# A small language-model block on one Trainium2 core: attention from fp32 heads on quarters of the array

## What is computed

```python
def _L0_attn_ref(x, qkv_w, qkv_b, proj_w, proj_b, q_norm_w, k_norm_w):
    qkv = x @ qkv_w.T + qkv_b                       # x: layernorm of h over the features
    q, k, v = split into 12 heads of 16
    q = rms_norm(q, q_norm_w);  k = rms_norm(k, k_norm_w)
    w = softmax(einsum('bhnd,bhmd->bhnm', q, k) / sqrt(16))
    out = einsum('bhnm,bhmd->bhnd', w, v)
    return out @ proj_w.T + proj_b                  # added to h
```

## Time and profile before

| | us |
|---|---|
| median of three runs (range) | 664.37 (664.18 to 664.48) |
| the profiled execution | 665.32 |
| its span, first to last instruction | 663.4 |
| mean granted TensorE clock, share of full speed | 0.928 |
| TensorE busy | 566.0 |
| VectorE busy | 377.8 |
| ScalarE busy | 271.9 |
| GpSimd busy | 84.3 |

### The profile page before, as it was taken

How to read it: one execution, slowest core, us unless ns; L and a number is a source line. 1 busy time by engine, 2 the same in 40 slices (tenths; PEclk the granted TensorE clock), 3 DMA queues, 4 the chain that set the end, 5 groups by cost and what they waited for, 6 DMA issues and landing times. The chain is left out here.

```text
span 663.4 us, 12309 instructions
## 1 busy us (share of the span) xinstructions
PE 566.0 (85%) x4521; PEld 460.8 (69%) x4521; DVE 377.8 (57%) x944; ACT 271.9 (41%) x787; POOL 84.3 (13%) x114
## 2 busy tenths in 40 slices
PE   6497896787999998988688777859988999999997
PEld 5386786764666666656376543548877999999996
DVE  2227648659899999988334653845662333223332
ACT  1123522344566666645325753514654222222220
POOL 5692000001000000000037400000100000000000
PEclk9799898999999999979687977967998999999999
DMA  9400000000000000000045002200003999999623
GB/s 316 121 1 2 0 1 1 0 1 1 1 2 1 1 0 0 1 1 1 1 171 223 1 1 84 96 0 1 2 1 124 404 311 313 306 318 309 217 47 108
DMA packets 20075, 57.90 MB, mean 87 GB/s; under 512 B 2804, under 2 KB 9574, under 8 KB 19911
## 3 DMA queue, kind: packets, MB, share of 16 engines
q1 hardware_dynamic: 14006, 48.04, 20.3%
q0 software_dynamic: 1024, 4.34, 3.6%
q10 hardware_dynamic: 4992, 4.82, 2.3%
HBM read 52.47 MB, written 4.33 MB: 86 GB/s over the span
## 5 line engine op out<-in xcount | busy, mean ns | idle before, releaser
L2048 DVE SCALAR_TENSOR_TENSOR ex_act_t<-banks,b_sb,ex_gelu 128x128 f32<-128x128 f32 x128 | 36.0, 344 | 95.4 <-ACT ex_gelu L2028 95.4
L2028 ACT ACTIVATE ex_gelu<-banks,b_sb 128x128 f32<-128x128 f32 x128 | 36.6, 368 | 100.7 <-PE banks L1979 100.7
L1974 PE MATMUL banks<-slots_t,w 128*128 128x128 f32 x512 | 62.5, 275 | 1.1 <-PEq L1670 1.1
L1974 PEld LDWEIGHTS banks<-slots_t,w 128*128 128x128 f32 x512 | 61.2, 192 | 1.4 <-issue 1.3
L1095 DVE TENSOR_REDUCE att_max<-banks 128x4 f32<-128x1024 f32 x48 | 58.6, 1220 | 2.6 <-PE banks L751 1.7
L945 ACT ACTIVATE att_prob<-banks 128x1024 f32<-128x1024 f32 x48 | 49.1, 1022 | 17.6 <-PE banks L774 17.6
L1992 PE MATMUL banks<-w,ex_act_t 128*128 128x192 f32 x256 | 50.2, 339 | 0.2 <-DVE ex_act_t L2048 0.2
L1992 PEld LDWEIGHTS banks<-w,ex_act_t 128*128 128x128 f32 x256 | 40.7, 189 | 4.3 <-DVE ex_act_t L2048 0.5
L1979 PE MATMUL banks<-slots_t,w 64*128 64x128 f32 x512 | 37.2, 285 | 0.0
L789 PE MATMUL banks<-att_prob,val 128*32 128x256 f32 x384 | 29.1, 426 | 7.2 <-ACT att_prob L945 7.0
L1187 POOL TENSOR_TENSOR att_qk<-att_qk,qk_weight 128x192 f32<-128x192 f32 x16 | 9.3, 600 | 203.8 <-DVE att_qk L1030 203.8
(11 more groups left out here) (233 smaller groups left out, 1144.0 us busy)
## 6 DMA issues: line engine op xcount, KB each, us to landing
w<-in_w SPq DMA_DIRECT2D x32, 768.0 KB, 7.7
w<-in_w2e SPq DMA_DIRECT2D x32, 384.0 KB, 8.6
w_slot<-in_w_slot SPq DMA_DIRECT2D x8, 576.0 KB, 3.8
rows_scratch<-ex_rows ACTq DMA_DIRECT2D x28, 96.0 KB, 6.5
yn_all<-rows_scratch POOLq DMA_DIRECT2D x7, 384.0 KB, 7.7
out<-h SPq DMA_DIRECT2D x8, 192.0 KB, 1.9
wq_t<-in_wq_t SPq DMA_DIRECT2D x1, 579.0 KB, 4.9
wk_t<-in_wk_t ACTq DMA_DIRECT2D x1, 579.0 KB, 5.4
```

What stands on the lines that cost most here:

```text
L1974: nc.tensor.matmul(bank[:, j * P:(j + 1) * P], g.w1[e][:, first + j * P:first + (j + 1) * P], x[:, 0, :], start=(j == 0), stop=False, skip ...
L2028: nc.scalar.activation(gelu[n % 2][:, j * P:(j + 1) * P], gate_bank(n)[:, j * P:(j + 1) * P], ACT.Gelu_apprx_tanh, bias=g.t["b1"][:, n, HB ...
L2048: nc.vector.scalar_tensor_tensor(out=act_t[n % 2][:, j * P:(j + 1) * P], in0=value_bank(n)[:, j * P:(j + 1) * P], scalar=g.t["b1"][:, n, j ...
```

## The change

The six bf16 parts are gone. The queries and keys of a head stay fp32, 16 features in a row of 32 columns (`g.qk`), and column 16 holds 1.0 for a key and, once `row_max` has run, the negated maximum for a query. A quad of four heads is then 128 columns, and one fp32 transpose lays head j on the partitions 32j to 32j+16. `fill_quad` has four such transposes a quad, for one bank of 128 x 512, and one copy a quad (ScalarE for quads 0 and 2, VectorE for quad 1). The scores are fp32 matmuls over 16 rows (for the maximum) or 17 rows (for the exponential), each on the quarter of the array's rows where its head lies. `scores_and_maxima` issues both kinds in turn, so that four matmuls in a row lie on four different quarters and write four different banks.

`split`, `split_rest`, `repeat` and `split_max` are removed on both engines. `turn_max` transposes the quad's 128 query columns again in fp32, and `keep_max` copies 128 x 256.

The 192 features of x are split as 128 + 64: three transposes of 128 columns give each tile its 128 and, in the third, the last 64 of both tiles on the two halves of the rows. The row of ones takes the place of feature 191: features of a normed row sum to zero, so GpSimd subtracts the weights' last row from all (`qkv_last`, in `token_mixer`), and the bias is loaded into the freed row by two DMAs that the attention stage waits for (`qkv_bias_set`). `keep_qk` is the two squares. Two operands, `qkv_w` (128 x 1728) and `qkv_last` (128 x 576), are loaded at the start in place of `qkv_t`.

The loops are written out in full, x is normalised two sequences ahead and not three, and the queries and keys are made one sequence ahead and not two. In the front part before body(0) only sequence 0 is made ready, with sequence 1's x; before, sequences 0 and 1 were made. The filler matmuls are at other places.

In the diff the first `body` is TensorE's, the second ScalarE's.

```diff
-            def max_scores(n, s, q, u):
-                pe.wait_ge(S["maxed"], 2 * count + u)
-                for hh in range(2):
-                    h = QH * q + 2 * u + hh
-                    for t in range(TPS):
-                        last = nc.tensor.matmul(g.ps[hh][:, t * SEQ:(t + 1) * SEQ],
-                                                q_t[s][0:KS, h, t * P:(t + 1) * P], k_t[s][0:KS, h, :],
-                                                start=True, stop=True)
...
+            def scores_and_maxima(score, best):
+                if score:
+                    n, q, u = score
+                    count = 2 * (QUADS * n + q) + u
+                    if u == 0:
+                        pe.wait_ge(S["max_kept"], QUADS * n + q + 1)
+                    if count:
+                        pe.wait_ge(S["exped"], count)
+                if best:
+                    bn_, bq, bu = best
+                    count = 2 * (QUADS * bn_ + bq) + bu
...
+                    if count:
+                        pe.wait_ge(S["maxed"], count)
+                for half in range(TPS):
+                    if best:
+                        for hh in range(2):
+                            row = 32 * (2 * bu + hh)
+                            last_best = nc.tensor.matmul(
+                                g.ps[MAXES[hh]][:, half * SEQ:(half + 1) * SEQ],
+                                g.qk_t[bn_ % 2][row:row + HDIM, bq, 0, half * P:(half + 1) * P],
+                                g.qk_t[bn_ % 2][row:row + HDIM, bq, 1, :], start=True, stop=True)
+                    if score:
+                        for hh in range(2):
+                            row = 32 * (2 * u + hh)
+                            last_score = nc.tensor.matmul(
+                                g.ps[SCORES[hh]][:, half * SEQ:(half + 1) * SEQ],
+                                g.qk_t[n % 2][row:row + HDIM + 1, q, 1, half * P:(half + 1) * P],
+                                g.qk_t[n % 2][row:row + HDIM + 1, q, 0, :], start=True, stop=True)
...
+            def body(n):
+                fill, stat, prev = n + 1 < BATCH, n + 2 < BATCH, n > 0
+                nxt = lambda q: (n, q + 1, 0) if q < QUADS - 1 else ((n + 1, 0, 0) if fill else None)
+                scores_and_maxima((n - 1, 2, 0) if prev else None, (n, 0, 1))
+                if fill:
+                    make_qk(n + 1)
+                scores_and_maxima((n - 1, 2, 1) if prev else None, nxt(0))
+                if fill:
+                    make_qk_rest(n + 1)
+                turn_max(n, 0)
+                if prev:
+                    mix(n - 1, 2)
+                scores_and_maxima((n, 0, 0), (n, 1, 1))
+                if prev:
+                    turn_out(n - 1)
+                scores_and_maxima((n, 0, 1), nxt(1))
+                if fill:
+                    make_v(n + 1)
+                turn_max(n, 1)
+                mix(n, 0)
+                if prev:
+                    turn_mixed(n - 1)
+                scores_and_maxima((n, 1, 0), (n, 2, 1))
+                if fill:
+                    fill_quad(n + 1, 0)
+                    fill_quad(n + 1, 1)
+                scores_and_maxima((n, 1, 1), nxt(2))
+                if fill:
+                    fill_quad(n + 1, 2)
+                if prev:
+                    project(n - 1)
+                turn_max(n, 2)
+                mix(n, 1)
+                if stat:
+                    turn_x(n + 2)
...
+            def body(n):
+                fill, stat, prev = n + 1 < BATCH, n + 2 < BATCH, n > 0
+                if prev:
+                    expo(n - 1, 2, 0)
+                    expo(n - 1, 2, 1)
+                if fill:
+                    keep_qk(n + 1)
+                if prev:
+                    keep_out(n - 1)
+                if fill:
+                    root_rms(n + 1)
+                expo(n, 0, 0)
+                if stat:
+                    root_var(n + 2)
+                expo(n, 0, 1)
+                if fill:
+                    keep_v(n + 1)
+                if prev:
+                    keep_mixed(n - 1)
+                expo(n, 1, 0)
+                if fill:
+                    keep_fill(n + 1, 0)
+                expo(n, 1, 1)
+                if fill:
+                    keep_fill(n + 1, 2)
+                if stat:
+                    keep_x(n + 2)
```

More of the change, by code:

```diff
@@ L30 @@
 QUADS, QH = 3, 4
-PARTS = 6
-KS = PARTS * HDIM
-KM = KS + 2 * QH
 SUM = HDIM
@@ new lines, in _ @@
+            pe.wait_ge(g.qkv_bias_set, 32)
+            keep_busy(nc, g, 0, 14)
+            turn_x(0)
+            keep_busy(nc, g, 0, 3)
+            make_qk(0)
+            make_qk_rest(0)
+            keep_busy(nc, g, 0, 6)
+            make_v(0)
+            keep_busy(nc, g, 0, 4)
+            turn_x(1)
+            keep_busy(nc, g, 0, 6)
+            for quad in range(QUADS):
+                fill_quad(0, quad)
+            scores_and_maxima(None, (0, 0, 0))
+            for n in range(BATCH):
+                body(n)
@@ L879, in _ @@
+            scores_and_maxima((BATCH - 1, 2, 0), None)
+            keep_busy(nc, g, 0, 3)
+            scores_and_maxima((BATCH - 1, 2, 1), None)
+            keep_busy(nc, g, 0, 4)
+            mix(BATCH - 1, 2)
+            keep_busy(nc, g, 0, 3)
+            turn_out(BATCH - 1)
+            keep_busy(nc, g, 0, 3)
+            turn_mixed(BATCH - 1)
+            keep_busy(nc, g, 0, 3)
+            project(BATCH - 1)
+            keep_busy(nc, g, 0, 6)
         @block.scalar
@@ L999, in _ @@
+            root_var(0)
+            keep_x(0)
+            root_var(1)
+            keep_qk(0)
+            root_rms(0)
+            keep_v(0)
+            keep_x(1)
+            keep_fill(0, 0)
+            keep_fill(0, 2)
+            for n in range(BATCH):
+                body(n)
+            expo(BATCH - 1, 2, 0)
+            expo(BATCH - 1, 2, 1)
+            keep_out(BATCH - 1)
+            keep_mixed(BATCH - 1)
         @block.vector
@@ L1181, in _ @@
+            norm_stats(0)
+            norm(0)
+            norm_stats(1)
+            norm(1)
+            sum_squares(0)
+            scale(0)
+            first_weigh()
+            keep_fill(0)
+            row_max(0, 0, 0)
+            for n in range(BATCH):
+                body(n)
+            divide(BATCH - 1)
+            add(BATCH - 1)
         @block.gpsimd
         def _(pool):
-            def weigh(n):
+            for t in range(TPS):
+                nc.gpsimd.memset(x[:, (t + 1) * DIM - 1:(t + 1) * DIM], 1.0).then_inc(S["ones_set"], 1)
@@ L1195, in body @@
-            def body(n, s, first=False, stat=True, make=True, fill=True):
-                if make:
-                    weigh(n + 2)
-            schedule(pool, prologue, body, lambda n, s: None)
 def first_slots(nc, g):
```

592 lines of the change are left out of this document (197 added, 395 removed).

## The result

The changed kernel takes 678.01 us in the median of four runs (672.6 to 681.11), the kernel before 664.42 (664.18 to 667.97; three of these four runs are those of the table before). The ratio is 1.0168, with a 95% interval of 1.013 to 1.0205. I had forecast 656 us and given slower a chance of 0.26: the direction is wrong.

What follows compares the result with a forecast made beforehand. VectorE was taken to bound attention bodies (21.0 of 21.8 us), then the chain through TensorE. Front part, bodies and rest, with handoffs, summed to 199.4 us for 208.25; 665.32 less 9 gave 656 us, range 645 to 681.

Steps and rivals of the forecast that it cites:

- The groups of scores: TensorE in attention: sixteen fp32 records a group, four at a time, 1.15 us until a reader may start.
- The first rival: Score groups: quarters overlap only in pairs or worse, 0.85 us more a group, 697 us; chance 0.13 with a milder form.
- The chain of a full body: Attention body, from one sequence's first score group to the next's: 20.8 us against 21.8.
- the steps G2 to G1: Between starts of a body's six score groups, second to next body's first: 3.5, 2.7, 4.15, 2.9, 5.0 us.
- what I added for handoffs: Attention bodies: 0.25 us a body for what comes second at each handoff.
- `keep_fill` ahead of G6: Body's sixth score group waits for a 0.58 us ScalarE copy behind the exponential; fifth to sixth group 2.9 us.
- Front part: Attention before body 0: about 20.2 us, 6 us less than 26.25.
- Body 0: First attention body, lacking the previous sequence's work: 19.3 us and 1 for a slow stretch, 20.3.
- Body 7 and the rest: End of attention, no new work filling TensorE: 28.5 us at full clock, 4.5 for lower clock, 33.0 against 31.4.
- The subtractions: GpSimd's three subtractions, beside TensorE work: cost nothing.
- Loads: At the start, 0.74 MB more, hidden by the gather: nothing, or 2.3 us if that cover is gone.
- The rival of the clock: Clock falls inside the bodies, 3.5 us per 7 us low stretch; one a body gives 680 us; chance 0.17.

Runs made afterwards that it cites:

- serial: Changed kernel with later subtractions and spare matmuls in bodies 0 and 7; each group's eight score records wait for its eight maxima records: 756.23 us, ratio 1.1331.
- light_front: As light, without the four spare matmuls ahead of the second sequence's transposes in the front part, three for six behind them: 657.23 us, ratio 0.9863.
- light: Changed kernel, subtractions after VectorE's additions for the first four sequences, fifteen spare matmuls in body 7, others in body 0: 654.20 us, ratio 0.9857.
- light_again: The kernel light once more, unedited, on the same chip as light_early: 656.79 us, ratio 0.9863.
- light_early: As light, but with the subtractions at once, beside VectorE's four additions, as in the changed kernel: 660.13 us, ratio 0.9922.
- fill_both: Changed kernel with spare matmuls in TensorE's gaps of body 7 and of body 0: 662.00 us, ratio 0.993.
- no_last: Changed kernel without the copy of the weights' last row (0.29 MB) and without the three subtractions: 673.78 us, ratio 1.0154.
- again: The changed kernel once more, no edit: 679.05 us, ratio 1.0192.
- after_again: The changed kernel once more, no edit, on the same chip as again: 680.60 us, ratio 1.023.
- padded old kernel: Kernel before the change with 15 spare matmuls, five ahead of each mixing of its last body: 662.60 us, ratio 0.9978.
- before_again: The kernel before the change, unedited, profiled again for its first stage on the chip of again and after_again; no median given.

## Why the prediction was wrong, step by step

**The groups of scores: right.** 1.15 us forecast, 1.14 in the trace; serial shows that the overlap is real and that the kernel needs it. The first rival (pairs or worse) did not come; its price of 697 us is not tested by serial's 756, which holds the low clock too. At full clock serial's body 7 with the rest grew by 5.9 us, some five groups at the 1.2 us by which one grew; the rival had 0.85. The Trainium skill, "TensorE: Matmul & The Clock Gate", Part 3, has 3.07 times for four row tiles. Here four records start every 0.21 us, and one alone would stream 0.213 (an estimate, twice the 0.107 of 128 columns): four times within a run of them, where 3.07 would have made it 0.28 (an estimate). Over the whole group, from its first record to the first of what follows (208.81 to 209.88, 1.07 us for the 3.4 of one at a time), it is 3.2 times.

**The chain of a full body: right to 0.4 us.** By the first records of the groups in body 2 (208.81, 212.56, 215.11, 219.50, 222.33, 227.41 us) the steps G2 to G1 are 3.75, 2.55, 4.39, 2.83 and 5.08, forecast 3.5, 2.7, 4.15, 2.9 and 5.0. With G1 to G2 a body has 21.2 us for 20.8, or 21.05 with what I added for handoffs. VectorE is busy for 13.5, for 14.5 in the sum: 7.5 us are gone and 0.6 came back. The waits are less right than the number. This is what ended TensorE's idle time in bodies 1 to 5 (total us, times, longest):

```profile
PE banks L736 <- ACT qk_t L914: 3.3, 5, 0.7
PE banks L736 <- DVE qk L1032: 3.0, 5, 0.6
PE banks L758 <- DVE qk L1032: 2.1, 5, 0.4
PE banks L664 <- DVE att_x L996: 1.7, 5, 0.3
```

`keep_fill` ahead of G6 and `norm` ahead of `turn_x` are as forecast. Ahead of `turn_max` and of G4 I had named the exponential; it is `row_max` (1.23 us for 1.02) that ends the wait, in body 2 by 0.15 and 0.05 us, so that the sum came out near all the same.

**Front part: 22.0 for 20.2**, 4.25 shorter than before where I said 6. The ten spare matmuls between `make_v` and the fill were in none of my terms; light_front could not show that they cost it. This stays open.

**Body 0: the step that failed first.** I gave it 19.3 and 1 for a slow stretch. Without low clock it has 20.2 (light, light_again, light_early, light_front). The change has 27.1 to 30.2. The step took the size of the slow stretch from the kernel before. That one has six spare matmuls at the start of its first body, where the scores of a previous sequence are missing (first row). The change has none there, and TensorE waits 1.33 us for `row_max` (second row). Both lie just ahead of `row_max(0, 0, 1)`, with which the stretch called body 0 begins:

```profile
152.53 1.50 PE L257 MATMUL banks<-ident 128*128 128x128 f32 x12
```

```profile
157.53 1.66 PE L736 MATMUL banks<-qk_t 16*128 16x256 f32 x8 [1.33 <-DVE qk L1032]
```

The granted clock is 1.00 from 141.0 to 158.0 us and 0.50 from 158.1 to 178.4; a second wait, of 1.41 us, lies inside that stretch. With eight spare matmuls in the place of the first wait, and eleven later, body 0 is back at 21.6 us (fill_both).

**Body 7 and the rest: the step that failed most.** Up to the last addition I had 28.5 at full clock and 4.5 for the lower one, 33.0. Up to the experts' start, 1 us later, this is 29.5 and 34.0; measured are 31.0 with the clock held and 42.6 in the change, so the low clock costs 11.6 where I had 4.5. The level was right (`mix` 1.94 again), but I took the share of the stage at the lower clock from the old kernel (a mean of 0.78, 0.79 up to the experts' start) although my own sum said that TensorE has less to issue. A mean of 0.64 is 72 per cent of the stretch at the lower level, for 42, and the fp32 groups, 2.08 us there for each eight records, all lie on the path. For the 28.5 itself the prediction shows no working; it was 1.5 too low, if the spare matmuls in the 31.0 cost nothing.

**The subtractions: wrong.** I wrote "beside TensorE work: nothing" and did not ask what VectorE does there. They cost 3.3 us by medians (light_early less light_again). In the trace three additions of 1.8 us each alternate with GpSimd's subtractions, and the fourth, when these are done, takes 0.54. The Trainium skill, "SBUF — State Buffer", section "Who interferes with whom", has the rule: a VectorE instruction with two SBUF inputs contends with a GpSimd instruction that reads SBUF. The trace agrees (5.63 us beside them, 1.97 ahead of them); by that rule I should have had up to the 4.12 us that the three take alone.

**Loads: not contradicted.** I had nothing; the first stage's delay goes with two of the chips, and no_last can't price the load closer than some 4 us.

**The rival of the clock** gave 680 us and the time came to 678, but not by its mechanism: it put the low stretches into the bodies, and those of bodies 1 to 6 have none in any kernel but serial. I wrote that a clock under 0.95 there would prove it; it is 1.00. Its price, 3.5 us for 7 us at the lower clock, was somewhat high: again has 10.0 us for a body 0 that is almost wholly low (30.2 us at 0.51), and the rest of the change 11.6 for 31 us (0.64 over 42.6). The place was the bodies at the ends, which have less work than the others. That 680 is so near the measured 678 is luck.

What ties them: after_again to light_again, on one chip, is 23.8 us by the table. The subtractions are 3.3 of it (light_early less light_again) and the clock of body 0 and of the rest 20.5 (after_again less light_early; their profiles have 10.0 in body 0 and 10.4 in the rest). What is left of the change without both is 8.4 us on the padded old kernel. That this is near the forecast's 9 is partly luck: the forecast counted 5.5 us of low clock in, and without them its attention stage is 193.9 us, where light_again has 197.9 up to the last addition.

Open: the experts' stages, which the change does not touch, took 321.4 us for 323.7. Over all profiles the change has 321.1 to 323.9 and the kernel before 323.7 to 324.3, so this may be the spread of their low stretches; it was not tried. That the clock holds when TensorE's idle time is filled is shown by adding work; whether the narrow matmuls of the new scores have a part in its fall was not tried.

## What to carry to other kernels

When a change takes work off TensorE, go through the first and the last trip of the software pipeline by themselves: there the overlapping stages are missing, and a clock that falls makes every TensorE step of what is left nearly twice as long (`mix` 1.94 us for 1.07). Spare matmuls in those gaps, as few as hold the clock, are the first thing to try (here 15 in place of 29 left the last body and the rest 0.9 us shorter, and 39 in the old kernel did harm). And a "free" instruction on GpSimd is to be set against what VectorE reads in that moment, not against TensorE.

## What I had not expected of the hardware

- The order in which matmuls for different quarters are issued made no difference: with eight for two quarters in front, the other two quarters started 0.03 us behind the first.
- Eight fp32 records of 256 columns on two quarters take 1.13 us, sixteen on four 1.14.
- On two of four chips the first stage ran late: a copy of VectorE that waits for TensorE ran at 17 to 18 us on two chips and at 26 to 31 on the others, in both kernels, with GpSimd's gathers and the loads under way. In before_again TensorE's matmul for it had ended at 17.8 us and the copy ran at 30.6. Why is open; the token mixer began some 1.7 us later.
- The additions of VectorE and the subtractions of GpSimd did not share: each of three additions took 1.8 us for 0.5.
